# Reordering one attention step: transposed scores before the values product, regrouping after the projections, ScalarE's exponential before its copies

## The reference, cut to what matters

```
Q, K, V = norm(x) @ Wq.T, ctx @ Wk.T, ctx @ Wv.T        # 16 heads of width 8
# layer 0: rotary embedding on Q and K; layer 1: 4 key/value heads, biases, causal and given mask
attn = softmax(Q K^T / sqrt(8));  out = attn @ V
x = x + out @ Wo.T           # layer 1: layernorm of out ahead of Wo
# layer 0 goes on with a quantised FFN, layer 1 with 8 experts, one for each token
```

## Time and profile before

| what | value |
| --- | --- |
| median of 3 runs | 578.75 us (578.5 to 578.78) |
| span of the profiled execution | 578.6 us |
| TensorE busy | 493.0 us (85%) |
| TensorE's weight loads | 361.9 us (63%) |
| VectorE busy | 399.0 us (69%) |
| ScalarE busy | 357.1 us (62%) |
| GpSimd busy | 372.8 us (64%) |
| mean granted TensorE clock | 0.964 |

### The profile page before, as it was taken

How to read it: one execution, slowest core, us unless ns; L and a number is a source line. 1 busy time by engine, 2 the same in 40 slices (tenths; PEclk the granted TensorE clock), 3 DMA queues, 4 the chain that set the end, 5 groups by cost and what they waited for, 6 DMA issues and landing times.

```text
span 578.6 us, 20130 instructions
## 1 busy us (share of the span) xinstructions
PE 493.0 (85%) x6238; PEld 361.9 (63%) x6239; DVE 399.0 (69%) x1248; ACT 357.1 (62%) x872; POOL 372.8 (64%) x755
## 2 busy tenths in 40 slices
PE   3587899999997799988999999999998834999993
PEld 2455666666665599976455555555554423999992
DVE  6687777777888578645578888888888762444441
ACT  4356677777766555653566776777765643666661
POOL 6868766676772367676556688888885561455552
PEclk9879999999999999999899999999999965999997
DMA  6664353534332860004433545444543114333330
GB/s 170 159 135 110 88 131 81 127 88 114 104 76 56 265 156 1 2 19 126 110 91 94 127 128 143 106 111 130 146 121 93 36 68 134 94 91 98 101 87 27
DMA packets 102161, 59.92 MB, mean 104 GB/s; under 512 B 20338, under 2 KB 98178, under 8 KB 102098
## 3 DMA queue, kind: packets, MB, share of 16 engines
q1 hardware_dynamic: 98738, 51.79, 35.5%
q0 software_dynamic: 2784, 6.82, 3.4%
q10 hardware_dynamic: 576, 0.53, 0.3%
HBM read 19.90 MB, written 8.81 MB: 50 GB/s over the span
## 4 chain that ended last, share of the span: by engine, by line
PE 47%; DVE 14%; issue 13%; SPq 8%; DMA 7%; POOL 5%; ACT 4%; ACTq 1%; DVEq 0%; POOLq 0%
DVE negmax L1448 6%; PE bank L688 6%; PE score L632 4%; PE bank L802 4%; PE scoreT L792 4%; DMA stack<-pieces 3%; PE bank L866 3%; PE bank L575 3%; PE bank L544 3%; SPq L404 3%; PE bank L703 2%; PE scoreT L854 2%; PE scoreT L661 2%; PE score L601 2%; SPq L470 2%
## 5 line engine op out<-in xcount | busy, mean ns | idle before, releaser
L1448 DVE TENSOR_REDUCE negmax<-score 128x8 f32<-128x1024 f32 x128 | 156.2, 1220 | 29.9 <-PE score L632 20.1
L975 ACT ACTIVATE P<-scoreT 128x1024 f32<-128x1024 f32 x128 | 131.0, 1024 | 40.1 <-PE scoreT L652 20.3
L688 PE MATMUL bank<-P,Vc 128*32 128x128 f32 x2048 | 82.7, 279 | 2.3 <-DVE product L1556 1.2
L632 PE MATMUL score<-stack 64*128 64x128 bf16 x1024 | 62.3, 221 | 15.6 <-DVE negmax L1448 9.5
L1337 POOL DMA_INDIRECT out<-by x39 | 40.2, 1031 | 51.3 <-issue 26.8
L632 PEld LDWEIGHTS score<-stack 64*128 64x128 bf16 x1024 | 33.6, 95 | 42.0 <-issue 23.1
L688 PEld LDWEIGHTS bank<-P,Vc 128*32 128x32 f32 x2048 | 48.6, 109 | 16.4 <-issue 4.3
L981 ACT COPY outs<-bank 128x256 f32<-128x256 f32 x64 | 23.7, 370 | 49.2 <-PE bank L688 49.2
L1199 POOL TENSOR_TENSOR pieces<-full,pieces 128x256 bf16<-128x256 f32 x63 | 42.2, 670 | 12.8 <-ACT pieces L956 12.8
L1202 POOL TENSOR_TENSOR pieces<-rest,pieces 128x256 bf16<-128x256 f32 x63 | 43.7, 693 | 4.9
L866 PE MATMUL bank<-M,bhT 128*128 x312 | 43.5, 282 | 0.3 <-ACT bhT L1102 0.3
(11 more groups left out here) (219 smaller groups left out, 1261.7 us busy)
## 6 DMA issues: line engine op xcount, KB each, us to landing
stack<-pieces SPq DMA_DIRECT2D x192, 128.0 KB, 2.5
ctxT<-in_ctxT SPq DMA_DIRECT2D x32, 128.0 KB, 2.4
XB<-expert_rows SPq DMA_DIRECT2D x39, 66.0 KB
XA<-expert_rows SPq DMA_DIRECT2D x39, 64.0 KB
XR<-in_x SPq DMA_DIRECT2D x4, 512.0 KB, 4.3
stack<-blank SPq DMA_DIRECT2D x32, 64.0 KB, 2.1
stack<-negpT SPq DMA_DIRECT2D x64, 32.0 KB, 1.9
M<-in_M SPq DMA_DIRECT2D x1, 2048.0 KB, 9.8
```

Of the source, the lines that this page charges most:

```text
L632: mm = nc.tensor.matmul(SCORE[:, r, i * 128:(i + 1) * 128], Qs[pb][rows, h, tb * S:(tb + 1) * S], Ks[pb][rows, kv, tb * S:(tb + 1) * S], s ...
L688: mm = nc.tensor.matmul(PVOUT[VCOL * i:VCOL * (i + 1), half * 128:(half + 1) * 128], Vc[:, k % BODY, at:at + VCOL], P32[:, c, i * 128:(i + ...
L975: nc.scalar.activation(P32[:, half * 2:half * 2 + 2, :], SCORET[:], ACT.Exp, scale=SCALE).then_inc(sem("exp_done"), 1)
L1448: nc.vector.tensor_reduce(negmax[:, k % 2, :, half * HQ:(half + 1) * HQ], SCORE[:].rearrange("p r (h k) -> p r h k", h=HQ), AX.X, ALU.max, ...
```

## The change

TensorE issues `scoresT(t, 0)` ahead of `pv(t-1, 1)` instead of behind it, and `regroup(t-1)` behind the two projections instead of ahead of them. ScalarE issues `exps(t, 0)` and `evac_max(t+1)` ahead of `evac_outs(t-1)` instead of behind it. No instruction is added or taken away, in either layer, and the lists of VectorE, GpSimd and SyncE stay as they are.

```diff
--- before
+++ after
@@ TensorE's step
                 def step(t, j):
                     scores(t + 2, 0, j + 2)
+                    scoresT(t, 0, j)
                     pv(t - 1, 1, j - 1)
-                    scoresT(t, 0, j)
                     max_transpose(t + 1)
                     out_transpose(t - 2)
-                    regroup(t - 1, j - 1)
                     if L and j % 2 == 0:
                         base_logits(j + 6)
                     project(j, 0)
                     project(j, 1)
+                    regroup(t - 1, j - 1)
                     scoresT(t, 1, j)
@@ ScalarE's step
-                    evac_outs(t - 1)
                     exps(t, 0)
                     evac_max(t + 1, j + 1)
+                    evac_outs(t - 1)
                     evac_out(t - 2)
                     exps(t, 1)
```

## The result

The changed kernel takes 607.6 us in the median (602.7 to 608.8, 4 runs) against 578.8 for the kernel before (578.5 to 582.0). The ratio is 1.0465, 95% interval 1.041 to 1.052: slower, as forecast, but by 28.8 us and not by 15, and outside the range, which ended at 602. The profiled execution has a span of 607.0 us at a mean granted TensorE clock of 0.950, against 578.6 at 0.964. In this and all later runs the whole time is about 1.8 us above the span.

A forecast was written before the change was run, and what follows sets the result against it. The prediction took a ring through the regrouping and VectorE's list behind it to bound the changed steps. 8.6 (layer 0) + 6.3 (layer 1) + 1.4 (last steps) - 1 (first steps) = 15.3 us, giving 594.0, range 584 to 602.

The forecast's parts named there:

- about 0.1 a step, 1.4 together: Last 7 steps of each layer: only ScalarE's order delays the regrouping, costing about 0.1 us a step, 1.4 together.
- TensorE's clock: TensorE throughout: the prediction had no term for a lower granted clock and so gave it no loss.
- layer 1's odd steps: Layer 1, odd steps: regrouping 0.83 us behind max_transpose, maxima at 2.60 against 2.49; taken as +0.08 us.
- Layer 0's steady steps: Layer 0, steps with projections: a pair of steps takes 10.71 us instead of 10.02, 8.6 us over 12.5 pairs.
- The ring through the regrouping: Layer 0: a later regrouping delays VectorE's list, the maxima and the next step, 3.02 us from regrouping to step.
- The deduction of 1 us for the first steps: First steps of layer 0: partly bound by late stacks, so 1 us was taken off the sum.
- The step from span to time: Whole kernel: the median of the runs was taken as 0.15 us above the profiled span.
- Layer 0 only: Rival: layer 1 loses nothing, TensorE's 0.1 us a step covering the rest; 586.4 or 587 us, 20%.
- The anchored odd step: Rival: layer 0's odd step stays tied to ScalarE's copies at 1.5 us, +1.3 a pair; 602 us, 17%.
- The other side: Rival: the ring does not pass through the regrouping, TensorE sets the step and the kernel gets faster; 568 us, 8%.
- the tiling rule of the Trainium skill: TensorE: a change of tiling mode drains it; one fewer a step saves 0.1 us, alone making the kernel faster.

The follow-up runs named there:

- B: Kernel before with only the regrouping moved behind the two projections on TensorE: 591.8 us, ratio 1.0191.
- A and B together: Changed kernel with ScalarE's order as before, evac_outs(t-1) ahead of exps(t, 0): 597.8 us, ratio 1.0308.
- C: Kernel before with only ScalarE's order changed, exps(t, 0) and evac_max(t+1) ahead of evac_outs(t-1): 686.8 us, no ratio given.
- rotate_first: Changed kernel with VectorE's rotations ahead of its reciprocal and normalisation in layer 0: 595.5 us, ratio 1.027.
- the filler's execution: Changed kernel with two unread weight products a step added on TensorE in steps 27 to 31 of layer 0: 603.0 us, ratio 1.041.
- A: Kernel before with only scoresT(t, 0) moved ahead of pv(t-1, 1) on TensorE: 590.3 us, ratio 1.0143.
- B and C: Changed kernel with scoresT(t, 0) behind pv(t-1, 1) as before: 640.2 us, ratio 1.106.

## Why the prediction was wrong

The direction and the mechanism of the steady steps held. What failed is the part of the sum outside them: the last steps at "about 0.1 a step, 1.4 together", and TensorE's clock, which had no term. The runs show some 2.7 us for the last steps at full clock, and 7 to 10 us of lost clock on top. A mis-sized term in layer 1's odd steps brings 2.3 us more.

**Layer 0's steady steps: right.** The ring through the regrouping, `outs`, and VectorE's list behind them is shown from three sides: B alone makes most of it (+0.41 us of the 0.65 a pair; A and B together +0.36, and C on top of them the rest), the rotations moved ahead take it away again, and TensorE waits for the maxima (negmax) in both parities. Forecast 10.71 a pair, measured 10.69 (10.82 in the two steps shown). That it is so near is in part luck, as two terms were off and cancel: the regrouping stands a little later (2.50 and not 2.37 in odd steps), and the way behind it is 2.91 and not 3.02.

**The deduction of 1 us for the first steps: wrong.** The first four intervals between regroupings of layer 0 are 26.7 us instead of 24.3, more than the 1.4 us of two steady pairs. The late stacks cover nothing there.

**Layer 1's odd steps: mis-sized.** I took 0.83 us from max_transpose to the regrouping, with the copy of the maxima waiting for that transpose alone. It waits for `out_transpose` behind it too (the wait stands in `evac_max`), and in layer 1 max_transpose comes late behind GpSimd. Measured 1.17; swapping the two transposes gives 0.95 and 2.0 us of the 2.3 by which the 25 steps were forecast too low. A pair costs 0.7 us on the mean of the 25 steps instead of 0.5: nearly nothing in the first seven steps, 0.9 in the later ones.

**The ends of both layers, "about 0.1 a step": mis-sized.** At full clock it is about 0.2 a step (28.8 instead of 27.4 us in layer 0, 32.9 instead of 31.6 in layer 1), so 2.7 us instead of 1.4. In layer 1 B alone has 32.0 us there and A with B 31.4, about as before, so C makes it: in these steps TensorE stands idle 0.67 us ahead of the regrouping, waiting for `outs`, and 0.2 us under A and B. Without projections nothing covers the time by which ScalarE's exponential delays `outs`. I had given this term no row; those of an exponential ahead of a copy gave 1.06 us.

**TensorE's clock: the largest miss, a term that the prediction put at nothing.** I took every TensorE duration at full clock, and gave the crossing to the FFN no loss. In the profiled execution the granted clock fell to half at the end of layer 0, in the crossing, and in the last six steps of layer 1. The same lists at full clock (rotate_first) take 3.9 us less in the last six steps of layer 0 and 2.3 less in those of layer 1. The crossing takes 1.0 less there and 3.6 less in the filler's execution, which has the full clock through all of it. So some 7 to 10 of the 28 us are the clock's in the profiled execution, most of the 13 that the forecast lacked. The other runs agree in sign: the changed kernel at 0.959 took 602.7 us, at 0.950 and 0.951 606.6 to 608.8.

**The step from span to time: off.** I set the time 0.15 us above the span, and it is about 1.8 in every later run; the span of 578.6 and the median of 578.75 are, as far as is known, of different executions.

**The rivals.** Layer 0 only is out: the change in layer 0 alone takes 595, and layer 1's steps then are as before. The anchored odd step (1.3 us a pair) is out: 0.65 was measured, and its total of 602 lies nearer to the result than the forecast by chance. The other side is out, and the tiling rule of the Trainium skill ("TensorEngine Tiling (Array Packing)", Key Properties) that spoke for it saves nothing in the total: A, the part that removes a change of tiling mode, gets max_transpose issued 0.1 us earlier and is slower alone, as TensorE then waits for `outs`.

**What stays open.** Why the clock fell isn't settled. It doesn't have to fall with the new order: in rotate_first TensorE stood idle in the same pieces ahead of the regroupings of the last steps (0.67 to 0.88 us) and kept the full clock. Whether the order makes a dip likelier isn't shown either: the fillers came too late for the first dip, one of their four runs had a low clock too, and the kernel before had one such execution. Over whole kernels the clock does go down where TensorE stands idle more: 0.943 to 0.970 in 40 executions of the kernel before, 0.920 to 0.943 in the four of B and C, 0.884 to 0.922 in the four of C alone. Why C alone costs nearly 4 us a pair in layer 1, what A alone costs outside the steady steps of layer 0, and why the stretch to the end is 1.8 us shorter, wasn't traced.

## What to carry to other kernels

Moving a piece behind others on one engine is free only if the engine that waits for it has nothing of the ring queued behind that wait: read the waiting engine's list up to the instruction that closes the ring, and add it up from the new place. Then look at the steps in which the moved piece's cover is missing (the first, the last), since a share of the loss sits there. Where a change adds idleness to TensorE in thin steps, price those steps at half clock too, as the upper end, and compare two kernels in a stretch only with the granted clock of that stretch beside each time.

## What the runs showed of the hardware

The same kernel on the same chip spreads with TensorE's granted clock: one variant took 581.5 us at 0.963 and 588.5 at 0.949. In that slower execution TensorE was at half its clock from 178 to 188 us, at 1.2 GHz instead of 2.4, and had stood idle in pieces of 0.5 to 0.7 us in the steps ahead. Such pieces alone don't decide it: rotate_first had pieces of 0.6 to 0.9 us in the same steps and stayed at full clock from 160 to 220 us. Identical lists of instructions in the last six steps of layer 1 took 35.2 us at a mean clock of 0.90 and 32.9 at 1.00. One or two per cent between two kernels of this kind can't be told by single executions.
